# The last query block's probabilities turned in 32x32 squares by VectorE, and the rotary embedding moved to GpSimd, in a fused attention and mixture-of-experts layer

## The reference

```
q, k, v = heads(x @ Wq), heads(x @ Wk), heads(x @ Wv)     # [8*16, 512, 64]
q, k    = apply_rope(q), apply_rope(k)     # (x1*cos - x2*sin, x1*sin + x2*cos) on even and odd entries
sim     = where(causal, q @ k.T / 8, -inf)
attn    = softmax(sim)
x       = layernorm(x + concat(attn @ v) @ Wo + bo)
top2    = top_k(softmax(x @ gate.T + expert_bias), 2)
x       = layernorm(layernorm(sum(w_e * (gelu(x @ Wup[e].T) @ Wdown[e].T))) + x)
```

## Time and profile before

| | before |
|---|---|
| median of 3 runs | 831.53 us |
| profiled execution, its own time | 833.04 us |
| its span, first to last instruction | 831.3 us |
| PE busy | 808.4 us, 97% |
| DVE busy | 671.6 us, 81% |
| ACT busy | 621.6 us, 75% |
| POOL busy | 391.7 us, 47% |
| mean share of 16 DMA engines on SP's queue | 25.8% |
| granted TensorE clock, mean | 0.998 |

### The profile page before, as it was taken

How to read it: one execution, slowest core, us unless ns; L and a number is a source line. 1 busy time by engine, 2 the same in 40 slices (tenths; PEclk the granted TensorE clock), 3 DMA queues, 4 the chain that set the end, 5 groups by cost and what they waited for, 6 DMA issues and landing times.

```text
span 831.3 us, 21041 instructions
## 1 busy us (share of the span) xinstructions
PE 808.4 (97%) x6267; PEld 591.3 (71%) x6267; DVE 671.6 (81%) x2590; ACT 621.6 (75%) x1672; POOL 391.7 (47%) x485
## 2 busy tenths in 40 slices
PE   8999999999999999999999999999999989999996
PEld 4566667666666666666666666666666669999995
DVE  6787798889888988899889988988898866123897
ACT  3677787888788878887788778878877766555577
POOL 3343433225433543343336533543363236989883
PEclk9999999999999999999999999999999999999999
DMA  4322312122322221222222222221123357434525
GB/s 145 121 84 89 109 58 85 62 76 74 102 71 82 75 91 69 78 78 77 77 77 77 78 77 77 77 90 65 68 81 112 113 142 206 129 84 129 159 81 157
DMA packets 75279, 78.62 MB, mean 95 GB/s; under 512 B 10336, under 2 KB 51040, under 8 KB 75168
## 3 DMA queue, kind: packets, MB, share of 16 engines
q1 hardware_dynamic: 70800, 68.42, 25.8%
q0 software_dynamic: 4224, 8.72, 3.1%
q10 hardware_dynamic: 144, 0.13, 0.1%
HBM read 28.39 MB, written 12.14 MB: 49 GB/s over the span
## 4 chain that ended last, share of the span: by engine, by line
PE 90%; DVE 4%; ACT 3%; issue 3%; DMA 1%; another core or an unknown queue 0%; SPq 0%; DVEq 0%; ACTq 0%
PE TB L1036 17%; PE S_all L989 17%; PE TB L1020 14%; PE S_all L1187 8%; PE AO L1057 7%; PE AO L1200 4%; PE TB L1200 4%; PE AO L918 3%; PE AO L916 3%; PE AO L917 3%; PE S_all L1020 2%; ACT PT L1317 2%; PE AO L980 1%; PE AO L979 1%; PE AO L978 1%
## 5 line engine op out<-in xcount | busy, mean ns | idle before, releaser
L1305 ACT ACTIVATE Pr_all<-Sm,nmax 128x512 f32<-128x512 f32 (+3 forms) x512 | 280.6, 554 | 1.4 <-DVE nmax L1520 1.4
L1520 DVE CUSTOM_DVE_ANT_0 Sm<-S_all,causal 128x512 f32<-128x512 f32 (+3 forms) x512 | 220.0, 487 | 67.7 <-PE S_all L989 67.6
L678 POOL TENSOR_TENSOR kT<-shared,kT 128x512 f32<-128x512 f32 x63 | 80.1, 1272 | 314.6 <-DMA kT<-shared 312.6
L1317 ACT ACTIVATE PT<-TB 128x1024 f32<-128x1024 f32 x185 | 131.0, 742 | 63.5 <-PE TB L1020 60.2
L989 PE MATMUL S_all<-kT,qT 64*128 64x512 f32 (+3 forms) x1024 | 166.9, 444 | 2.7 <-DVE nmax L1520 2.1
L1036 PE MATMUL TB<-PT,shared 128*64 128x128 f32 x1008 | 149.8, 438 | 5.3 <-ACT PT L1317 0.3
L1541 DVE SCALAR_TENSOR_TENSOR x_acc<-AO,rinv,x_acc 128x128 f32<-128x128 f32 x504 | 141.7, 344 | 3.9 <-remote 1.5
L1020 PEld LDWEIGHTS TB<-ident,Pr_all 128*128 128x128 f32 x1000 | 108.0, 141 | 38.4 <-ACT Pr_all L1305 21.4
L1020 PE MATMUL TB<-ident,Pr_all 128*128 128x128 f32 x1000 | 133.8, 277 | 0.5 <-ACT PT L1317 0.5
L989 PEld LDWEIGHTS S_all<-kT,qT 64*128 64x128 f32 x1024 | 79.1, 187 | 72.0 <-issue 55.2
L1036 PEld LDWEIGHTS TB<-PT,shared 128*64 128x64 f32 x1008 | 69.3, 136 | 58.0 <-issue 38.6
(11 more groups left out here) (319 smaller groups left out, 1337.5 us busy)
## 6 DMA issues: line engine op xcount, KB each, us to landing
kT<-shared SPq DMA_DIRECT2D x124, 128.0 KB, 2.0
qT<-shared SPq DMA_DIRECT2D x124, 128.0 KB, 2.0
wo<-in_wo SPq DMA_DIRECT2D x64, 64.0 KB, 1.9
PT<-yrows SPq DMA_DIRECT2D x7, 512.0 KB
w_tile<-in_wup SPq DMA_DIRECT2D x10, 256.0 KB
xt<-xrows SPq DMA_DIRECT2D x32, 65.0 KB
x_acc<-in_x SPq DMA_DIRECT2D x8, 256.0 KB
wdown<-in_wdown SPq DMA_DIRECT2D x8, 256.0 KB
```

Source lines behind the costliest of these rows:

```text
L678: nc.gpsimd.tensor_tensor(kT[p][:, :], k_cos, kT[p][:, :], ALU.add).then_inc(k_ready, 1)
L1305: nc.scalar.activation(Pr[j][:, 0:n], Sm[j], ACT.Exp, bias=nmax[:, j:j + 1], scale=-1.0, accum_out=rsum[p][:, h * QB + qb:h * QB + qb + 1] ...
L1317: last = nc.scalar.activation(PT[p][:, :, 0:qb + 1, qb * P:qb * P + P], source, ACT.Copy)
L1520: nc.vector.tensor_tensor_reduce(out=Sm[j], in0=SB[2 * (group % 2) + h][:, at:at + n], in1=causal[:, T - n:T], scale=-0.125, scalar=HUGE, ...
```

## The change

Three things are done together.

1. **Group 0 leaves PE.** For all units but the last, DVE transposes the two 512-wide blocks of the last query rows in 32x32 squares (`turn`, a STREAM_TRANSPOSE of 128x512) into `turned_pr`. A square lies in the right columns but in the wrong group of 32 partitions, so SP writes the tile to a DRAM buffer `turns` (one DMA, 512 KB) and loads it back in four DMAs of 32 partitions each (128 KB, pieces of 1 KB) straight into `PT`. `attend` waits for these loads (`turns_in`). The layout of `PT` becomes [blocks of 32 queries, 2 x key block + head, 32], so that its matmuls read 32 contiguous elements at a time, 1 KB apart.
2. **The banks move.** Groups 1 and 2 both go through `TB`; `attend` writes the bank `AB`, and `project_q` writes the second bank of `TB` right behind group 2.
3. **The embedding moves.** From unit 2 on, ACT copies the projected keys and queries from PSUM to `k_cos` and `q_cos` (`keep_k`, `keep_q`). POOL multiplies the keys by sin and cos (`turn_k`). DVE multiplies the queries by sin (`rope_q`, now with both inputs in SBUF), then POOL multiplies them by cos (`scale_q`). Keys and queries are swapped together by two DMAs of 256 KB, and POOL adds both in the next step, ahead of the next `turn_k`. `norm_x1` moves one unit later.

The final FFN buffer `f_acc` has its own name for memory that attention has given up; nothing of the expert phase changes.

where the store is ahead of the swap, and the loads, which wait for the store to land, behind it. The core of the diff:

```diff
             # SP
+            def store_turned(u, p):
+                sp.wait_ge(turned, 2 * u + 2)
+                wait(sp, turns_in, LOADED * (u - 1))
+                sp.dma_start(turns[p * P:p * P + P, :], turned_pr[:, :, :, :].rearrange("p b c s -> p (b c s)")).then_inc(stored, 16)
+            def load_turned(u, p):
+                sp.wait_ge(stored, 16 * (u + 1))
+                wait(sp, pv_done, u - 1)
+                squares = turns[p * P:p * P + P, :].rearrange("(a r) (b n) -> b r a n", r=SQ, b=LANES)
+                for b in range(LANES):
+                    sp.dma_start(PT[p][SQ * b:SQ * b + SQ, LANES * (QB - 1):, :, :].rearrange("k a c s -> k a (c s)"),
+                                 squares[b]).then_inc(turns_in, 16)
+            def swap(u, p):
                 sp.wait_ge(k_read, u + 1)
+                sp.wait_ge(q_read, u + 1)
                 wait(sp, scored, BLK * (u - 1))
+                sp.dma_start(qk[p][0:P:2, :, :], qk_rot[1:P:2, :, :]).then_inc(swapped, 16)
+                sp.dma_start(qk[p][1:P:2, :, :], qk_rot[0:P:2, :, :]).then_inc(swapped, 16)
...
             # POOL
+            def turn_k(u):
+                pool.wait_ge(k_kept, u - PLAIN + 1)
+                nc.gpsimd.tensor_tensor(k_rot, k_cos, sin_t[:, :], ALU.mult)
+                nc.gpsimd.tensor_tensor(k_cos, k_cos, cos_t[:, :], ALU.mult).then_inc(k_read, 1)
+            def scale_q(u):
+                pool.wait_ge(q_read, u + 1)
+                nc.gpsimd.tensor_tensor(q_cos, q_cos, cos_t[:, :], ALU.mult).then_inc(q_scaled, 1)
...
-                if batch > 0 and n == NORM_AT:
+                if batch > 0 and n == NORM_AT + 1:
                     norm_x1(batch - 1)
...
+                if PLAIN <= u + 1 < UNITS:
+                    rotate_k(u + 1, 1 - p)
+                    rotate_q(u + 1, 1 - p)
                 if u + 2 < UNITS:
-                    rotate_k(u + 2, p)
-                    rotate_q(u + 2, p)
+                    turn_k(u + 2)
+                    scale_q(u + 2)
...
             # PE
             def attend(u, p):
                 pe.wait_ge(v_ready, QB * (u // VS + 1))
-                pe.wait_ge(pt_ready, 3 * u + (1 if u == UNITS - 1 else 2))
+                pe.wait_ge(turns_in, LOADED * (u + 1))
+                if u < UNITS - 1:
+                    pe.wait_ge(k_kept, min(u + 2, UNITS - PLAIN))
...
             # ACT
+            def keep_k(u):
+                act.wait_ge(k_proj, u + 1)
+                act.wait_ge(k_ready, u)
+                nc.scalar.activation(k_cos, k_bank(u), ACT.Copy).then_inc(k_kept, 1)
+            def keep_q(u):
+                act.wait_ge(q_proj, u + 1)
+                act.wait_ge(q_ready, u)
+                nc.scalar.activation(q_cos, q_bank(u), ACT.Copy).then_inc(q_kept, 1)
...
+                exp(u, p, 0)
+                exp(u, p, 1)
                 if not first:
-                    copy_pt(u - 1, 1 - p, 0)
+                    copy_pt(u - 1, 1 - p, 1)
+                if u + 2 < UNITS:
+                    keep_k(u + 2)
                 if 1 <= u <= VBLOCKS - QB:
                     copy_v(QB + u - 1)
                 if not first:
-                    copy_pt(u - 1, 1 - p, 1)
                     copy_pt(u - 1, 1 - p, 2)
-                exp(u, p, 0)
-                exp(u, p, 1)
+                if u + 2 < UNITS:
+                    keep_q(u + 2)
+                for j in range(FIRST_OF[1], FIRST_OF[2]):
+                    exp(u, p, j)
...
             # DVE
+            def turn(u, h):
+                dve.wait_ge(exped, BLK * u + h + 1)
+                wait(dve, stored, 16 * u)
+                nc.vector.transpose(turned_pr[:, :, h:2 * QB:2, :].rearrange("p b k s -> p k b s"),
+                                    Pr[h].rearrange("p (k b s) -> p k b s", b=LANES, s=SQ)).then_inc(turned, 1)
...
-                for j in range(2, BLK):
+                for j in range(FIRST_OF[1], FIRST_OF[2]):
                     mask_max(u, j)
+                if not last:
+                    for h in range(2):
+                        turn(u, h)
+                for j in range(FIRST_OF[2], BLK):
+                    mask_max(u, j)
+                if not first and u + 2 < UNITS:
+                    rope_q(u + 2)
...
-                if u + 2 < UNITS:
-                    rope_k(u + 2)
-                    if not first:
-                        rope_q(u + 2)
```

More of the change, by code:

```diff
@@ L3 @@
 from contextlib import ExitStack
+from itertools import accumulate
 F32 = mybir.dt.float32
@@ L30 @@
 SWAPPED = 2 * 16
+SQ = 32
+LANES = P // SQ
+LOADED = LANES * 16
 VS = 4
@@ L145, in sb, with in_turn @@
             return ctx.enter_context(nc.sbuf_tensor(name, shape, dtype))
+        def in_turn(first, then):
+            with ExitStack() as attention_only:
+                held = [attention_only.enter_context(nc.sbuf_tensor(*of)) for of in first]
+            return held, sb(*then)
         def ps(name, shape=(P, 512)):
@@ L179, in build_block @@
         wo = [sb(f"wo{i}", [P, C]) for i in range(2)]
-        qT = [sb(f"qT{i}", [P, T]) for i in range(2)]
-        kT = [sb(f"kT{i}", [P, T]) for i in range(2)]
+        qk = [sb(f"qk{i}", [P, 2, T]) for i in range(2)]
+        qT, kT = ([qk[i][:, which, :] for i in range(2)] for which in range(2))
         shared = sb("shared", [P, 3 * QB * VS * P + PAIRS * P])
@@ L192, in build_block @@
         Sm = [Sm_of[qb][:, h, :] for h, qb in ORDER]
-        Pr_all = sb("Pr_all", [P, BLK, T])
-        Pr = [Pr_all[:, i, :] for i in range(BLK)]
+        (Pr_all, turned_pr), f_acc = in_turn(
+            [("Pr_all", [P, QB * (QB + 1) * P], F32), ("turned_pr", [P, LANES, 2 * QB, SQ], F32)], ("f_acc", [P, NT, C], F32))
+        ends = list(accumulate((qb + 1) * P for h, qb in ORDER))
+        Pr = [Pr_all[:, end - (qb + 1) * P:end] for end, (h, qb) in zip(ends, ORDER)]
         nmax = sb("nmax", [P, BLK])
@@ L1151, in attention @@
                 if not first:
-                    transpose(u - 1, 1 - p, 1)
+                    transpose(u - 1, 1 - p, 2)
+                if u + 2 < UNITS:
+                    project_q(u + 2, *second)
                 if batch > 0 and n == TURN_AT:
@@ L1764, in attention @@
                 mask_max(u, 1)
-                if u < 2:
-                    (rope_k, rope_q)[u](u + 1)
+                if u == 0:
+                    second_k()
+                if u == 1:
+                    rope_q(2)
                 if u >= 2:
                     scale_y(u - 2)
-                for j in range(2, BLK):
+                for j in range(FIRST_OF[1], FIRST_OF[2]):
                     mask_max(u, j)
+                if not last:
+                    for h in range(2):
+                        turn(u, h)
+                for j in range(FIRST_OF[2], BLK):
+                    mask_max(u, j)
+                if not first and u + 2 < UNITS:
+                    rope_q(u + 2)
                 if u == 1:
```

191 lines of the change are left out of this document (93 added, 98 removed).

## The result

The changed kernel takes 847.87 us (median of 4 runs, 846.22 to 848.51), the kernel before 831.8 beside it: a ratio of 1.0185, 95% interval 1.016 to 1.021. I had predicted 796 us in a range of 775 to 828. The sign was wrong, and no rival of mine is what happened.

A forecast was written before the change was run, and what follows sets the result against it. The prediction took PE, 97% busy, to bound the kernel: 833.0 less 57 for PE's transposes, plus 9 (POOL's loop), 10 (`norm_x1`) and 3 (late units, counts) gave 798, or 796 us as median, range 775 to 828.

The forecast's parts named there:

- no rival of mine: Whole kernel: all hidden 0.20; POOL's loop binds every unit 0.17; DRAM trip binds, or slow PT reads or turn, 0.15.
- DVE's unit of 8.7 us "of 9.3": DVE in attention: its unit of 9.16 us loses 0.5 and becomes 8.7, within PE's 9.3.
- a floor of 9.3: PE in attention: its work per unit, 10.2 us before, becomes 9.3 us without group 0's transposes.
- 3 us for late units and counts: SP waiting for late expert weights ahead of `store_turned` (units 58 to 62), and POOL counting tiles: 3 us added.
- PE's loss of 0.9 us a unit: PE in attention: group 0's transposes go, 0.9 us in each of 63 units, 57 us in all.
- The turn: DVE's transpose in squares, two a unit: 0.65 us each from start to start, bounds 0.55 and 1.28.
- PT in pieces of 32 elements: Attend's reads of PT, 1 KB apart: costed at nothing; 2.3 us a unit were reads twice as long.
- The loop through DRAM: Scores, turns, store, loads, attend, two units long: 9.0 us a unit likely, bounds 7.5 and 11.6; likely hidden.
- My 7.8 for L: Store to DRAM and loads back: estimated with a 3.2 us store by the skill's fit; 8.5 us was the likely value.
- POOL's loop and `norm_x1`: POOL's additions, products and swap, likely 9.2 us a unit: 9 us late; `norm_x1` not fitting: 10 us.
- the lock: DVE instructions with two SBUF inputs wait for POOL strings reading SBUF; 0.5 us added at `rope_q`.
- the slower side of my chances, 0.15: Whole kernel slower: DRAM round trip binds (about 877 us), or PT pieces or a slow turn (few per cent); together 0.15.

The follow-up runs named there:

- The kernel of fills: Changed kernel with POOL's three products a unit each replaced by two write-only fills: 805.74 us, ratio 0.9697 against the kernel before.
- the repaired kernel: Changed kernel with queries multiplied on DVE from PSUM, SP's loads of expert weights issued later, and POOL's tile counting two units later: 803.63 us, ratio 0.9662.
- the repaired kernel with short products: Kernel with the three repairs (queries on DVE, SP's order, later counting), POOL's key products cut to 64 of 512 columns: 790.97 us, ratio 0.9518.
- The repaired kernel with fills: Kernel with the three repairs (queries on DVE, SP's order, later counting), POOL's key products replaced by write-only fills: 793.21 us, ratio 0.9546.

## Why the prediction was wrong, step by step

- **The step that failed: DVE's unit of 8.7 us "of 9.3".** I saw the mechanism, foresaw `rope_q` at 1.1 to 1.3 us (it is 1.31) and wrote that "some routing instructions behind it wait for `scale_q`", but priced the whole at 0.5 us, took it as hidden in the slack of 0.6, and put nothing of it into the sum. Measured: 0.62 us a unit in `rope_q` and 40 us over the kernel in small instructions, 78.6 / 62 = 1.27 us a unit. With the 8.7 that is 10.0 against a floor of 9.3, so DVE became the bound. The kernel of fills gives its price, 42 us (with POOL busy 0.9 us a unit less in it), nearly the 50 us by which the profiled execution (848.5) is over my 798.
- **3 us for late units and counts** was mis-sized. SP's order costs 6 to 10 us, 5.7 of them in unit 61. Unit 43 is some 10 us over its neighbours, and 41 and 42 some 2 us each; I do not have these apart from the other repairs, as no run moves POOL's counting alone.
- **PE's loss of 0.9 us a unit** was right: where nothing is late, masks stand 9.15 us apart, and the repaired kernel with short products averages 602.8 / 63 = 9.57.
- **The turn** at 0.65 from start to start, 1.30 for two: right. **PT in pieces of 32 elements** at no cost: right, attend keeps its 2.37 us (one is shown below).
- **The loop through DRAM**, hidden: right, at most 4 us, and of these 1.3 in unit 61. In the repaired kernel with short products several units in a row take 9.2 us, so the loop is no longer than that; I had 9.0. My 7.8 for L by the fit in the Trainium skill's "DMA: Bandwidth & Descriptors" (Anatomy of one DMA) does not come out of my own terms, 3.2 + 1.7 + 2.6 = 7.5. That section also gives the fit for DMAs of GpSimd, and these are SP's. Nothing in the sum rests on it.
- **POOL's loop and `norm_x1`**, 19 us: probably too much. The swap's landing was right (2.5 us for 256 KB, 317.87 to 320.36). PE, which I had waiting at attend for `keep_k`, does so six times from 80 to 560 us, 4.3 us in all. In the repaired kernel, whose loop lacks `scale_q`, a chain shorter by 1.4 us a unit brings 2 us. In the changed kernel itself the loop can't be told apart from the lock, since `rope_q` waits for POOL's products.
- The repaired kernel with fills is at 793.2, against 796 less the 3 us. That agreement is partly luck: its queries are on DVE and its POOL chain is shorter than the one I priced.

Attend in the changed kernel, with its 32-element reads:

```profile
315.04 2.37 PE L1083 MATMUL AO<-PT,shared 128*64 128x128 f32 x16
```

The sign came out wrong because the slower side of my chances, 0.15, held only the DRAM trip and the pieces. That POOL would go from 47% to near 85% busy in attention was in my own text (it is 372 of 480 us, 78%); what it does to each DVE instruction with two SBUF inputs was priced for one instruction and not for all of them.

## What to carry to other kernels

Before work moves to POOL, list every DVE instruction whose inputs are both in SBUF, the short ones first, and look at copies and scalings within SBUF too. Charge each the rest of the POOL instruction or string that it may meet, not its own length. Here the query products were cheaper both on DVE from a bank (815 us) than halved between two engines that read SBUF (848 us). On an in-order queue, what the next unit needs goes ahead of loads that are needed later.

## What the runs showed of the hardware that I had not expected

- A blocked DVE instruction can wait through several adjoining POOL instructions: 0.19 us became 4.53 across four of them, one of which was an indirect DMA's 1.10 us, and 15 of the `rope_q` took 1.93 to 1.99 us. It need not: twelve took 0.69 to 0.75. What decides is open.
- POOL's fills of 128x512 (526 ns) leave a DVE product beside them at 690 ns; POOL's products leave it at 1311.
- Both sides pay: where DVE comes first, POOL's product takes 1.73 us instead of 1.28. Here in the changed kernel DVE gets in between L720, which ends at 306.04, and L721:

```profile
305.86 0.72 DVE L1549 TENSOR_TENSOR shared<-shared,sin_t 128x512 f32<-128x512 f32 x1 [1.27 <-ACT shared L1372]
305.99 1.73 POOL L721 TENSOR_TENSOR shared<-shared,cos_t 128x512 f32<-128x512 f32 x1
```

- In a stall of PE of 4.4 us the granted clock fell to its lower level and stayed there for the 16 matmuls behind it (0.50 from 659 to 665 us), so a late transfer was paid about half again in slower matmuls: 2.2 us on top of 4.4.
